# Inverse root by Newton steps on VectorE for two groups at once, all scaling on GpSimd, bias in four pieces between the turnings

## The reference, cut to what matters

```python
def step(h, _):                       # 30 times; ln_w = 1, ln_b = 0, EPS = 1e-5
    h = h + 0.01 * jnp.tanh(h)
    h = h * jax.nn.sigmoid(h)
    mu = jnp.mean(h, axis=-1, keepdims=True)
    var = jnp.mean(jnp.square(h - mu), axis=-1, keepdims=True)
    h = (h - mu) * jax.lax.rsqrt(var + EPS) * ln_w + ln_b
    h = jnp.einsum('bsc,dc->bsd', h, W) + b
    return (h, None)
h, _ = jax.lax.scan(step, layernorm(x), None, length=30)
out = x + h                           # x: (16, 512, 128)
```

## Time and profile before

| | us |
|---|---|
| median of three runs (1292.48 to 1292.98) | 1292.58 |
| span of the profiled execution, first to last instruction | 1290.6 |
| graph part, to the first step of the recurrence in PSUM | about 557 |
| recurrence, from there to the end | about 734 |
| VectorE busy over the span | 1190.1 (92%) |
| TensorE busy over the span | 1258.6 (98%) |
| ScalarE busy | 1006.7 (78%) |
| GpSimd busy | 961.9 (75%) |

### The profile page before, as it was taken

One profiled execution on the slowest core, in us unless ns is written; L12 is line 12 of the kernel. 1 busy time (PEld: TensorE's weight loads), 2 busy tenths in 40 slices (PEclk: granted clock), 3 DMA queues, 4 the chain that ended last, 5 costly groups with the idle time before them and its releaser, 6 DMA issues.

```text
span 1290.6 us, 29533 instructions
## 1 busy us (share of the span) xinstructions
PE 1258.6 (98%) x9309; PEld 1122.3 (87%) x9309; DVE 1190.1 (92%) x2808; ACT 1006.7 (78%) x1410; POOL 961.9 (75%) x783
## 2 busy tenths in 40 slices
PE   8899999999999999699999999999999999999998
PEld 7677777777777777499999999999999999999998
DVE  7988888888888877899999999999999999999997
ACT  2455555555555555799999999999999999999995
POOL 2455545554455554499999999999999999999996
PEclk9999999999999999899999999999999999999999
DMA  6111111111111000000000000000000000000004
GB/s 192 42 42 41 44 50 55 50 46 41 41 41 41 0 1 1 1 2 1 0 0 0 0 0 0 0 0 0 0 0 0 0 0 0 0 0 0 0 0 131
DMA packets 29810, 27.74 MB, mean 21 GB/s; under 512 B 3285, under 2 KB 21464, under 8 KB 29656
## 3 DMA queue, kind: packets, MB, share of 16 engines
q1 hardware_dynamic: 29784, 27.41, 6.7%
HBM read 23.21 MB, written 4.19 MB: 21 GB/s over the span
## 4 chain that ended last, share of the span: by engine, by line
PE 82%; DVE 10%; ACT 3%; issue 3%; POOL 0%; DMA 0%; SPq 0%; DVEq 0%; ACTq 0%; POOLq 0%
PE psum L865 33%; PE psum L881 16%; PE psum L861 7%; PE psum L634 4%; PE psum L636 4%; PE psum L635 4%; PE psum L805 4%; PE psum L656 3%; PE psum L651 3%; DVE emb_n L1415 2%; DVE xh_mem L1239 1%; PE psum L645 1%; ACT emb_f L999 1%; PE psum L665 1%; DVE upd L1376 1%
## 5 line engine op out<-in xcount | busy, mean ns | idle before, releaser
L485 POOL TENSOR_TENSOR f_rs<-f_var,half_neg 128x8 f32<-128x8 f32 x240 | 397.1, 1655 | 20.3 <-DVE f_var L1305 1.8
L865 PEld LDWEIGHTS psum<-w_t,y_all 128*128 128x128 f32 x2880 | 382.7, 193 | 9.3
L865 PE MATMUL psum<-w_t,y_all 128*128 128x128 f32 x2880 | 388.6, 275 | 0.0
L1268 DVE BATCH_NORM_STATS2 f_stat<-g_ring 128x6 f32<-128x256 f32 x960 | 341.4, 417 | 2.4 <-ACT g_ring L936 2.4
L491 POOL TENSOR_TENSOR h_ring<-g_ring,f_rs 128x640 f32<-128x640 f32 x240 | 302.0, 1259 | 18.8
L1280 DVE SCALAR_TENSOR_TENSOR u_ring<-t_ring,psum 128x1024 f32<-128x1024 f32 x232 | 278.9, 1202 | 0.0
L936 ACT ACTIVATE g_ring<-u_ring 128x1024 f32<-128x1024 f32 x240 | 264.5, 1103 | 1.7 <-DVE u_ring L1280 1.6
L959 ACT ACTIVATE y_all<-psum 128x1024 f32<-128x1024 f32 x240 | 254.2, 1059 | 8.8 <-PE psum L881 8.8
L881 PE MATMUL psum<-ident,h_ring 128*128 128x128 f32 (+1 forms) x1920 | 251.5, 274 | 2.4 <-issue 2.4
L946 ACT ACTIVATE t_ring<-psum 128x1024 f32<-128x1024 f32 x232 | 245.9, 1060 | 0.8 <-PE psum L865 0.8
L881 PEld LDWEIGHTS psum<-ident,h_ring 128*128 128x128 f32 (+1 forms) x1920 | 231.3, 154 | 3.0 <-issue 2.9
(11 more groups left out here) (194 smaller groups left out, 2137.0 us busy)
## 6 DMA issues: line engine op xcount, KB each, us to landing
work<-in_adj_dram SPq DMA_DIRECT2D x16, 1024.0 KB, 5.4
x_tok<-in_x_dram SPq DMA_DIRECT2D x16, 256.0 KB, 5.5
out_dram<-y_all SPq DMA_DIRECT2D x7, 512.0 KB, 3.2
work<-in_L_gnn_conv_w_dram SPq DMA_DIRECT2D x1, 1088.0 KB
out_dram<-y_all SPq DMA_DIRECT2D x2, 256.0 KB, 3.5
work<-in_L_gnn_w_ih_dram SPq DMA_DIRECT2D x1, 384.0 KB
work<-in_L_gnn_w_hh_dram SPq DMA_DIRECT2D x1, 192.0 KB
work<-in_L_gnn_W_dram SPq DMA_DIRECT2D x1, 64.0 KB, 5.2
```

Source lines behind the costliest of these rows:

```text
L485: pool.tensor_tensor(f_rs[:, j % 4, :], f_var[:, j % 2, :], half_neg[:, 0:GT], ALU.pow).then_inc(f_pow, 1)
L865: m = pe.matmul(y_ps[k % 2][:, h, C * t:C * t + C], y_all[:, GT * k + NT * h + t, :], w1_t[:] if t < biased else w1c_t[:], start=False, st ...
L1268: ins = dve.bn_stats(f_stat[:, j % 4, 0, 2 * q:2 * q + 2, :].rearrange("p t w -> p (t w)"), both)
```

## The change

`power` and its GpSimd instruction go, except for the first four groups of iteration 0. VectorE computes the inverse roots of sixteen tiles (two groups) by eight small instructions (`root_link`): the sum of the partial variances, a first guess from the bits of the number, and three Newton steps. The sixteen variances and the guesses live in PSUM bank 7; `share` multiplies guess, variance and guess (three rows of sixteen numbers), `better` makes two copies of the next guess from it. In the loop `bias_free` waits for the u of the group before (`f_u >= it * GROUPS + k`). The eight links are laid one by one between the four statistics instructions, five in an odd slot and three in an even one. `silu` and statistics now lag one slot.

GpSimd scales all eight tiles of a group in two instructions of four tiles. Scaling on ScalarE and VectorE, the second weight and the row of ones go. `g_ps[0]` and `g_ps[1]` now share bank 5, so the second half of a turning waits for the copy of the group before. The bias of the next group goes in front, as four products of 256 columns between the eight turnings.

```diff
-LAG_S = 2
-LAG_V = 3
-LAG_P = 4
-LAG_A = 5
+LAG_S = 1
+LAG_P = 5
 LAG_T = 6
...
-        g_ps = [psum[:, 4 + 2 * r:6 + 2 * r, :] for r in range(2)]
+        g_ps = [psum[:, 4 + r:6 + r, :] for r in range(2)]
+        root = psum[:, 7, 0:5 * PAIR].rearrange("p (w t) -> p w t", t=PAIR)
+        VAR = 2
+        GUESS = [(1, 3), (0, 4)]
...
-                t = GT - ACT_TILES[j] - DVE_TILES[j]
-                pool.tensor_tensor(tiles(h_ring[j % 4])[:, 0:t, :], tiles(g_ring[j])[:, 0:t, :],
-                                   spread(f_rs[:, j % 4, 0:t], t, C), ALU.mult).then_inc(f_norm, 1)
+                for h in (j % 2, 1 - j % 2):
+                    at = GT * (j % 2) + NT * h
+                    pool.tensor_tensor(tiles(h_ring[j % 4])[:, NT * h:NT * h + NT, :], tiles(g_ring[j])[:, NT * h:NT * h + NT, :],
+                                       spread(f_rs[:, both(j), at:at + NT], NT, C), ALU.mult).then_inc(f_norm, 1)
...
+            def bias(k, part):
+                h, c = part // 2, part % 2
+                pe.matmul(y_ps[(k + 1) % 2][:, h, 2 * C * c:2 * C * c + 2 * C], ones_bf[:],
+                          bias1[:, 0:2, :].rearrange("p t c -> p (t c)"),
+                          start=(c == 0), stop=False, skip_group_check=True)
...
+                for n in range(GT):
+                    if before is not None:
+                        if n == NT:
+                            pe.wait_ge(f_norm, 2 * s + 2)
+                            if ends(i, 0) and j == 0:
+                                pe.wait_ge(s_x_nmp_lo, B)
+                            else:
+                                pe.wait_ge(f_state, s)
+                        t = (n + NT * (j % 2)) % GT
+                        m = pe.transpose(g_ps[j % 2][:, t // NT, P * (t % NT):P * (t % NT) + P],
+                                         tiles(h_ring[j % 4])[:, t, :], ident[:])
+                    if ahead and n % 2 == 0:
+                        if n == 0:
+                            bias_free(it, k)
+                        bias(k, n // 2)
...
+            def share(n, done):
+
+                rows = root[:, GUESS[n][0]:GUESS[n][1] + 1:VAR - GUESS[n][0], :].rearrange("p w t -> p t w")
+                dve.wait_ge(f_link, done)
+                dve.tensor_reduce(f_share[:], rows, AX_X, ALU.mult).then_inc(f_link, 1)
+
+            def better(n, less, done):
+
+                dve.wait_ge(f_link, done)
+                dve.scalar_tensor_tensor(out=guess(1 - n), in0=twice(f_share[:]), scalar=less,
+                                         in1=twice(root[:, GUESS[n][0], :]), op0=ALU.subtract, op1=ALU.mult).then_inc(f_link, 1)
```

More of the change, by code:

```diff
@@ L22 @@
 F32R = mybir.dt.float32r
+I32 = mybir.dt.int32
 ALU = mybir.AluOpType
@@ L378, in exists, with both, pairs @@
             return b is not None and not (isinstance(b, int) and b == B)
[L380 to L386, removed]
+        def both(j):
+            return j // 2 % 2
+        def pairs(i, j):
+            return i * (GROUPS // 2) + j // 2 - BY_POWER // 2
         def ends(b, last):
@@ L569, in _ @@
             steps(pool, step)
-            slots(pool, slot)
+            slots(pool, slot, EARLY, 2)
         @block.tensor
@@ new lines, in product_group @@
+            def product_group(it, k):
+                s = (it - 1) * GROUPS + k
+                pe.wait_ge(f_state, s + 1)
+                for h in range(2):
+                    for t in range(NT):
+                        m = pe.matmul(y_ps[k % 2][:, h, C * t:C * t + C], y_all[:, GT * k + NT * h + t, :], w1_t[:],
+                                      start=False, stop=True, skip_group_check=True)
+                    if h == 0 and ends(it, ITERS) and k == GROUPS - 1:
+                        m.then_inc(f_half, 1)
+                m.then_inc(f_mm, 1)
@@ L877, in slot @@
-                    wait(pe, f_state, s - 1)
-                    for t in range(GT):
-                        rows = P if t < GT - DVE_TILES[j] else P - 1
-                        m = pe.transpose(g_ps[j % 2][0:rows, t // NT, P * (t % NT):P * (t % NT) + P],
-                                         tiles(h_ring[j % 4])[:, t, 0:rows], ident[:])
+                    pe.wait_ge(f_norm, 2 * s + 1)
+                    if ends(i, 0) and j < 2:
+                        pe.wait_ge(*((s_conv_pre, B) if j == 0 else (s_r, B)))
+                    else:
+                        pe.wait_ge(f_state, s - 1)
@@ L883, in slot @@
+                if before is not None:
                     m.then_inc(f_turn, 1)
-            pe.wait_ge(s_ones, 1)
             slots(pe, slot, LAG_T, 2)
@@ L962, in slot @@
             def slot(it, k):
+                if not ends(it, ITERS):
+                    tanh(it, k)
                 before = earlier(it, k, LAG_S)
@@ L965, in slot @@
                     silu(*before[1:])
-                if not (isinstance(it, int) and it == ITERS):
-                    tanh(it, k)
-                before = earlier(it, k, LAG_A)
-                if before is not None:
-                    scale(*before[1:])
                 before = earlier(it, k, LAG_T)
@@ L1317, in slot @@
                     scaled_sum(it, k)
-                before = earlier(it, k, LAG_V)
-                if before is not None:
-                    variance(*before[1:])
+                older = earlier(it, k, LAG_ROOT + (k + 1) % 2)
+                first, last = (0, 5) if k % 2 else (5, LINKS + 1)
+                if older is not None and first < last:
+                    root_link(first, *older)
+                before = earlier(it, k, LAG_S)
+                for q in range(GT // 2):
+                    if before is not None:
+                        statistics_of(*before[1:], q)
+                    if older is not None and first + 1 + q < last:
+                        root_link(first + 1 + q, *older)
             def conv_sum(b):
```

193 lines of the change are left out of this document (92 added, 101 removed).

## The result

The changed kernel takes 1303.4 us, median of four runs (1303.05 to 1303.53), against 1292.5 for the kernel before in the same comparison: ratio 1.0086, 95% interval 1.0072 to 1.0100. It is 10.9 us slower; the forecast was 1257 and its range ended at 1283. The span of the profiled execution is 1301.1 us, at a granted clock of 0.997.

A forecast was written before the change was run, and what follows sets the result against it. VectorE was taken as the bound at 3.066 us a slot, TensorE 0.07 behind; 231 x (3.066 - 2.92) = 33.7, plus 1.3 and 0.8, gave 35.8 us saved and a forecast of 1257, range 1247 to 1283.

The forecast's parts named there:

- a piece costs 0.06: TensorE between turnings: each 256-column bias product adds 0.06 us, four 0.24; slot 2.64 + 0.24 = 2.88, with hand-overs 2.89.
- the other argument: TensorE bias weights: their load is short, since behind a wait the next load starts 0.01 later.
- VectorE 2.87: VectorE per slot: keeps 2.45 us of u and statistics, gains four links at 0.105 each, 0.42.
- links at 0.13 and more: Rival on VectorE: links bound the slot; 0.13 each gives 1268, 0.16 gives 1296; chance 0.15 for 0.12 and more.
- 0.16 a link: VectorE estimate from the skill page, charging PSUM operations 120 cycles: slot near 3.05, about 1287 us.
- GpSimd 1.01 a half: GpSimd scaling: each 512-column half takes 1.01 us by columns, at most 1.26; two halves 2.0 to 2.5.
- The new waits fit: TensorE: bias piece's wait for u and turning's wait for state fit, by 0.4 and 0.2 us.
- The fifth turning's wait for the shared bank: TensorE waits for the previous group's state, done about 2.05, load at 2.23; shared-bank rival 1275, chance 0.08.
- VectorE and TensorE close together, 0.03 for that: Slot: TensorE 2.89 and VectorE 2.87 are close and odd and even slots differ, so 0.03 is added: 2.92.
- Outside the slots: Outside the 231 slots: 1.3 us won where the graph part ends, 0.8 us in the last iteration.
- The bias is not hidden: Rival on TensorE behind turnings 1, 3, 5, 7: each piece costs 0.115, slot 3.10, 1298 us; chance 0.10.

The follow-up runs named there:

- the bf16 turnings: Changed kernel with six of the eight turnings of a slot as bf16 of half the channels, output meaningless: 1256.0 us, ratio 0.9718, slot 2.913.
- two pieces: Changed kernel with only two of the four bias pieces a slot, output meaningless: 1255.6 us, ratio 0.9719.

## Why the prediction was wrong

Step by step, by its own sum:

- **TensorE, a piece costs 0.06: wrong, and the one step that failed.** It measured 0.11, four cost 0.44 and not 0.24, and with 2.67 for the other 24 instructions (I had 2.64) the sum is 3.11 in place of 2.89. The sentence was: "A turning streams for only 0.06; in a queue of turnings the 0.11 is the load of the next tile." It came from the earlier trace rows, where the first of four turnings after an idle stretch costs 0.06 more. That row says only that 0.11 and 0.06 are the two parts. It doesn't say which is which, and I took the wrong one: by the runs above the moving is the 0.11, and what an exposed load adds is the 0.06.
- **The row that would have told was there.** In the earlier trace rows a bias product of 512 columns has a record of 0.39 and one of 256 columns 0.27: a record grows by 0.11 to 0.12 for 256 columns. Turnings have 0.27 as well. With 0.06 of moving it would have been 0.22, as the bf16 turnings have. The start-to-start distance can't part the load from the columns, the record's length can.
- **Another row of that trace says it by distance.** In the graph part, float32 passes (128 x 128 weights, each with its load) move 512 columns:

```profile
498.00 3.60 PE L805 MATMUL psum<-work,msg_tok 128*128 128x512 f32 x8
```

Their record is 0.59, so eight starts lie (3.60 - 0.59) / 7 = 0.43 apart, four times the 0.11 of a turning for four times the columns. With the load as the price of a turning the two would have no reason to stand in that ratio. (Products of the type float32r, such as L634, also print as f32 in these rows and take 0.23 for 512 columns; which is which stands in the kernel.)

- ****, the other argument, was read rightly and proves nothing: the load of the bias weights is short, but what holds a piece back is the moving of the turning in front of it, not the piece's load.
- **VectorE 2.87: right.** Links measured 0.39 a slot where I had 0.42, statistics 1.36 for 1.33, u 1.14 for 1.12; 2.89. The rival of links at 0.13 and more fell: PSUM on both sides costs no more than the row of 36 columns said, and no wait on `f_link` is seen. The estimate from the Trainium skill's page "VectorE: DVE Perf Modes", 0.16 a link, is not borne out: 0.07 to 0.11.
- **GpSimd 1.01 a half: right**, 1.00. The gap is 1.1 us a slot.
- **The new waits fit: right.** The fifth turning's wait for the shared bank never shows; the first piece's wait for u is 1.1 us in the whole run.
- **VectorE and TensorE close together, 0.03 for that: right in size by luck.** With two pieces the slot is 2.911, 0.02 over the sums, but not because two engines are close: the u's stand 2.77 and 2.99 apart in turn, 2.88 on average, and 3.24 once in eight where the hardware loop turns. The forecast had no term for that turn.
- **Outside the slots: half right.** The start of the recurrence won 1.7 for a forecast of 1.3; since the first u stands anywhere from 554.7 to 556.3 in the versions run here, the agreement says little. The last iteration lost 2.0 where I had a gain of 0.8. That gain followed from TensorE at 0.1 less a slot, and TensorE had 0.12 more. But with two pieces, where TensorE did have 0.1 less, there was no gain either: the forecast left out that the products now start later relative to the last u, 1.6 us in the changed kernel.
- **The rival "The bias is not hidden"** had the mechanism, the place, the slot (3.10, measured 3.11) and the sign. It gave 1298; the slot (0.01 longer, 2.3 us) and what lies outside the slots (0.3 lost where it counted 2.1 won) make up the difference about equally. I gave it one chance in ten, where the case against it rested on one row that has two readings; even odds would have been fair.

## What to carry to other kernels

Where a start-to-start distance could be load or moved columns, read the lengths of the records as well: they grow with what is moved, and two widths of one operation in the same profile give the slope. Work that is spread between other instructions of an engine is hidden only if the neighbours leave the resource free that it needs; here piece and turning both needed the columns' time, and 1024 columns cost 0.44 us in either place. When an engine has slack (GpSimd, 257 us), use it to take work off the bound one, but price the exact form of the instruction first.

## What the runs showed of the hardware

- A float32 turning of 128 columns takes 0.109 to 0.112 us of TensorE, a bf16 one 0.055 to 0.06, and a bf16 product of 128, 256 and 512 columns 0.06, 0.11 and 0.22; the mean granted clock was 0.992 to 0.997 of the upper level, 2.4 GHz, in all these runs. A float32 pass of a product, 128 columns, takes 0.11 like the turning.
- Records of weight loads: 192 ns for a float32 product, 141 for a turning of 128 float32 channels, 190 for one of 127, 111 for one of 64, 97 to 98 for bf16. In a full queue the long ones are seen only behind an instruction that moves for less than 0.11: 127 channels behind a 128-column piece cost 0.05, and so does a product behind a bf16 turning. The Trainium skill, "TensorE: Matmul & The Clock Gate", section on Fast Weight Load, has loads faster only where there are 128 weights of a type other than float32. The 97 of bf16 agrees; the 141 against 190 of turnings, 128 against 127 channels, is a float32 case that it doesn't have.
- Going from 65 rows to 64, or from 64 to 128, takes 0.20 to 0.21 us to the next start in place of 0.11, and from 64 to 65 it takes 0.155; two turnings of 64 rows in a row stand 0.112 apart. Changing between 65 and 128 costs nothing that shows.
- GpSimd takes 0.77 us for 128 columns with two scalars per token, 1.00 for 512 columns of a two-input operation with a broadcast operand, and a record of 0.83 for 384 columns.
